# A two-layer model on one core: `weigh` of the second chunk moved behind its scan, and the first step's weight pieces and engine orders changed

## What is computed

```python
zxbcdt = hidden @ W_in                       # 2 x 1024 tokens, 512 -> gate 1024, x 1024, B 16, C 16, dt 16 heads
xBC = silu(conv4(xBC) + conv_b)              # causal, four taps
dt = softplus(dt + dt_bias)
dA = exp(dt * -exp(A_log))
for t: h = h * dA[t] + (dt[t] * x[t]) B[t];  y[t] = h C[t]      # per head, 64 x 16 state
y = (y + D_skip * x) * silu(gate)
y = y * rsqrt(mean(y * y) + 1e-5) * norm_w
out = y @ W_out;  x = layernorm(x + out)
```

## Time and profile before

| | |
|---|---|
| time, median of 3 runs | 1096.6 us (1095.79 to 1098.11) |
| the profiled execution's own time | 1097.13 us |
| its span, first to last instruction | 1095.4 us |
| TensorE busy | 1040.9 us (95%) |
| VectorE busy | 710.6 us (65%) |
| ScalarE busy | 576.1 us (53%) |
| the first layer | the first 400 us: a first step of 61 us, then steps of 48.1 us |
| mean granted clock of TensorE | 0.99 |

### The profile page before, as it was taken

One profiled execution on the slowest core, in us unless ns is written; L12 is line 12 of the kernel. 1 busy time (PEld: TensorE's weight loads), 2 busy tenths in 40 slices (PEclk: granted clock), 3 DMA queues, 4 the chain that ended last, 5 costly groups with the idle time before them and its releaser, 6 DMA issues.

```text
span 1095.4 us, 17774 instructions
## 1 busy us (share of the span) xinstructions
PE 1040.9 (95%) x6784; PEld 911.9 (83%) x6784; DVE 710.6 (65%) x1217; ACT 576.1 (53%) x1189; POOL 343.6 (31%) x465
## 2 busy tenths in 40 slices
PE   5799999999999977999999999899999999999997
PEld 5688889898988966899999999788888888888886
DVE  5999989999998988676677678854341142233123
ACT  7968686776868664566556655663203312321320
POOL 1014324241432415343534353323313312321331
PEclk9999999999999998999999999999999999999999
DMA  7421221404132452401100110435012012001001
GB/s 269 142 91 51 104 98 55 141 11 150 44 110 77 151 166 76 183 1 39 39 25 16 39 39 24 128 110 212 1 48 68 1 39 77 1 13 65 1 1 58
DMA packets 41332, 81.18 MB, mean 74 GB/s; under 512 B 7200, under 2 KB 13216, under 8 KB 39200
## 3 DMA queue, kind: packets, MB, share of 16 engines
q1 hardware_dynamic: 41248, 80.05, 21.6%
HBM read 67.18 MB, written 12.85 MB: 73 GB/s over the span
## 4 chain that ended last, share of the span: by engine, by line
PE 65%; DVE 18%; ACT 7%; issue 4%; POOL 3%; DMA 2%; SPq 0%; DVEq 0%; POOLq 0%; ACTq 0%
PE banks L1859 21%; PE banks L810 17%; PE banks L1872 11%; PE banks L1507 7%; DVE a_L L674 4%; PE banks L1475 4%; DVE c_gx L1366 1%; PE banks L926 1%; DVE c_cv L1342 1%; DVE a_xs L705 1%; DMA c_xb<-tokens 1%; PE banks L874 1%; DVE c_xb L1321 1%; ACT c_a L1241 1%; DVE a_ex L660 1%
## 5 line engine op out<-in xcount | busy, mean ns | idle before, releaser
L1759 ACT ACTIVATE d_sg<-banks,d_gs 128x512 f32<-128x512 f32 x64 | 44.0, 688 | 224.9 <-PE banks L1859 224.9
L1802 DVE SCALAR_TENSOR_TENSOR d_h<-banks,d_us,d_sg 128x512 f32<-128x512 f32 x64 | 48.0, 750 | 163.7 <-PE banks L1859 151.4
L1733 POOL TENSOR_TENSOR d_hl<-d_h,d_hh 128x512 fp32r<-128x512 f32 x64 | 83.4, 1303 | 158.1 <-ACT d_hh L1763 158.1
L1872 PE MATMUL banks<-d_wd,d_hh 128*128 128x512 f32 x256 | 101.1, 395 | 0.0
L1872 PE MATMUL banks<-d_wd,d_hl 128*128 128x512 f32 x256 | 100.9, 394 | 0.0
L649 DVE SCALAR_TENSOR_TENSOR a_xs<-a_xpre,a_cvec,a_xs 128x256 f32<-128x256 f32 x192 | 91.7, 543 | 1.0 <-ACT a_xs L454 1.0
L810 PE MATMUL banks<-a_xth,a_wxh 128*128 128x256 f32 x256 | 74.8, 292 | 2.7 <-DVE a_wxl L585 2.7
L674 DVE TENSOR_TENSOR_SCAN a_L<-a_L,a_ident 128x512 f32<-128x512 f32 x64 | 74.7, 1210 | 0.5
L810 PE MATMUL banks<-a_xth,a_wgh 128*128 128x256 f32 x256 | 74.6, 291 | 0.0
L341 POOL TENSOR_TENSOR a_sg<-a_sg 128x512 f32<-128x512 f32 x16 | 20.6, 1290 | 169.4 <-ACT a_sg L446 169.4
L810 PE MATMUL banks<-a_xtl,a_wxh 128*128 128x256 f32 x256 | 72.6, 284 | 0.0
(11 more groups left out here) (273 smaller groups left out, 3106.6 us busy)
## 6 DMA issues: line engine op xcount, KB each, us to landing
a_L<-decays SPq DMA_DIRECT2D x16, 1024.0 KB, 4.7
a_xf<-in_x_turned SPq DMA_DIRECT2D x16, 256.0 KB, 4.0
a_xr<-in_x SPq DMA_DIRECT2D x16, 256.0 KB, 2.8
tokens<-a_xr SPq DMA_DIRECT2D x16, 256.0 KB, 2.1
c_xb<-tokens SPq DMA_DIRECT2D x16, 256.0 KB, 3.1
d_xin<-tokens SPq DMA_DIRECT2D x16, 256.0 KB, 4.9
d_r<-tokens SPq DMA_DIRECT2D x16, 256.0 KB, 2.6
d_wd_codes<-in_down_w SPq DMA_DIRECT2D x4, 1024.0 KB, 9.4
```

Of the source, the lines that this page charges most:

```text
L1733: pool.tensor_tensor(hl[:, m, :], h32[:, m % 2, :], hh[:, m, :].bitcast(F32), ALU.subtract).then_inc(s_hl, 1)
L1759: act.activation(sg[:, m % 2, :], ps_g[:, m % 2, :], ACT.Silu, scale=gs[:, m:m + 1]).then_inc(s_sg, 1)
L1802: dve.scalar_tensor_tensor(out=h32[:, m % 2, :], in0=ps_u[:, m % 2, :], scalar=us[:, m:m + 1], in1=sg[:, m % 2, :], op0=ALU.mult, op1=ALU. ...
L1872: ins = pe.matmul(ps_o[:, c % 2, :], h[:, m, cols(c)], wd[:, m, :], start=(m == 0 and h is hh), stop=(m == M - 1 and h is hl))
```

## The change

In all steps, `weigh` of the second chunk stands directly behind its scan on VectorE, ahead of `update`, `output` and `conv_bc`. All else is in the first step:

- The pieces of w_x and of the gate's weights are column blocks: piece 1 + p holds the 256 columns that `x_proj(0, p)` needs, with all 512 input rows, in runs of 1 KB. `x_proj(0, p)` and `gate(0, p)` wait for their own piece.
- ScalarE and VectorE split two x pieces, then do `nega`'s exponential and clamp and ScalarE's `bc(0)`, then the other two; the first eviction stands ahead of softplus and decay.
- TensorE turns the steps' dt behind `x_proj(0, 3)`, does `gate(0, 0)` ahead of the first `x_turn`, and `gram(0)` behind it; VectorE takes the turned dt (`steps_in`) behind its third convolution pair.
- The four w_out pieces are split at the end of step 0's order: on ScalarE ahead of `high_y(0)`, on VectorE ahead of `low(0)`.

```diff
--- before.py
+++ after.py
@@ -201,19 +201,18 @@
 
     pieces = [(w_bc.rearrange("(k p) n -> p k n", p=P), wb[0], wb[1], KD, None)]
     for w_dram, w in ((w_x, wx), (w_gate, wg)):
-        for k in range(KD):
-            pieces.append((w_dram[k * P:(k + 1) * P, :], w[0][:, k, :], w[1][:, k, :], 1, None))
+        for p in range(4):
+            own = slice(2 * p * P, (2 * p + 2) * P)
+            pieces.append((w_dram.rearrange("(k p) n -> p k n", p=P)[:, :, own], w[0][:, :, own], w[1][:, :, own], KD, None))
     for m in range(0, M, 2):
         pieces.append((w_out[m * P:(m + 2) * P, :].rearrange("(a p) n -> p a n", p=P), wo[0][:, m:m + 2, :], wo[1][:, m:m + 2, :], 2, m))
-    NX, NG, NW = 1 + KD, 1 + 2 * KD, len(pieces)
+    NX, NG, NW = 5, 9, len(pieces)
     for raw, src, hi, lo in following:
         pieces.append((src, hi, lo, None, None))
     def staged(i):
         w, n = pieces[i][1], pieces[i][3]
         if n is None:
             return following[i - NW][0]
-        if n == 1:
-            return stage[i % 4]
         return stage[i % 4][:, 0:n * w.shape[2]].rearrange("p (a n) -> p a n", a=n)
 
     def chunk(dram, s, j):
@@ -497,17 +496,19 @@
 
         high_piece(0)
         turn(0)
-        for i in range(1, NX):
-            high_piece(i)
+        high_piece(1)
+        high_piece(2)
+        act.wait_ge(s_prep, 1)
+        act.activation(nega, nega, ACT.Exp).then_inc(s_prep, 1)
         act.wait_ge(s_small, 64)
         bc(0)
+        high_piece(3)
+        high_piece(4)
+        act.wait_ge(s_const, 15 + HQ)
+        evict(0, 0)
         softplus(0)
-        act.wait_ge(s_prep, 1)
-        act.activation(nega, nega, ACT.Exp).then_inc(s_prep, 1)
         act.wait_ge(s_prep, 3)
         decay(0)
-        act.wait_ge(s_const, 15 + HQ)
-        evict(0, 0)
         high_piece(NX)
         high_piece(NX + 1)
         evict(0, 1)
@@ -541,9 +542,6 @@
             else:
                 following_stage["turn_in"](0)
                 high_piece(NW)
-            if s == 0:
-                for i in range(NG, NW):
-                    high_piece(i)
             own_heads(C * s)
             if s:
                 normalize(C * s - 2)
@@ -560,6 +558,9 @@
                 evict(s + 1, 1)
             else:
                 following_stage["square"](0)
+            if s == 0:
+                for i in range(NG, NW):
+                    high_piece(i)
             high_y(C * s)
         square(C * NS - 2)
         following_stage["softplus"](0)
@@ -719,14 +720,15 @@
 
         low_piece(0)
         turn(0)
-        for i in range(1, NX):
-            low_piece(i)
+        low_piece(1)
         dve.wait_ge(s_small, 64)
         dve.tensor_scalar(nega, nega, LIMIT, None, ALU.min).then_inc(s_prep, 1)
+        low_piece(2)
         dve.wait_ge(s_prep, 2)
         dve.tensor_scalar(nega, nega, -1.0, None, ALU.mult).then_inc(s_prep, 1)
+        low_piece(3)
+        low_piece(4)
         conv_bc(0)
-        steps_in(0)
         dve.wait_ge(s_const, 15 + HQ)
         for s in range(NS):
             conv_pair(s, 0)
@@ -742,7 +744,9 @@
             else:
                 mean_sq(C * s - 2)
             conv_pair(s, 2)
-            if s:
+            if s == 0:
+                steps_in(0)
+            else:
                 residual(C * s - 2)
             conv_pair(s, 3)
             scan(C * s, 0)
@@ -761,16 +765,13 @@
             else:
                 following_stage["turn_in"](0)
                 low_piece(NW)
-            if s == 0:
-                for i in range(NG, NW):
-                    low_piece(i)
             scan(C * s + 1, 1)
+            weigh(C * s + 1)
             update(C * s)
             output(C * s, 0)
             output(C * s, 1)
             if s + 1 < NS:
                 conv_bc(s + 1)
-            weigh(C * s + 1)
             mix(C * s + 1, 0)
             mix(C * s + 1, 1)
             if s + 1 == NS:
@@ -779,6 +780,9 @@
             update(C * s + 1)
             output(C * s + 1, 0)
             output(C * s + 1, 1)
+            if s == 0:
+                for i in range(NG, NW):
+                    low_piece(i)
             low(C * s)
             if s + 1 < NS:
                 steps_in(s + 1)
@@ -855,8 +859,8 @@
             pe.matmul(ps_q[:, j:j + 1], sg[:, 0, cols(j)], ones, start=True, stop=True).then_inc(s_sp, 1)
 
         def x_proj(s, p):
-            if s == 0 and p == 0:
-                pe.wait_ge(s_wlo, NX)
+            if s == 0:
+                pe.wait_ge(s_wlo, 2 + p)
             if p < 2:
                 wait(pe, s_sg, 4 * (s - 1) + p + 3)
             else:
@@ -875,8 +879,8 @@
             last.then_inc(s_xtr, 1)
 
         def gate(s, p):
-            if s == 0 and p == 0:
-                pe.wait_ge(s_wlo, NG)
+            if s == 0:
+                pe.wait_ge(s_wlo, NX + 1 + p)
             if p < 2:
                 pe.wait_ge(s_acc, M * s + 2 * p + 6)
             else:
@@ -931,7 +935,6 @@
         pe.wait_ge(s_wlo, 1)
         bc(0)
         x_proj(0, 0)
-        turn_steps(0)
         x_proj(0, 1)
         for s in range(NS):
             x_proj(s, 2)
@@ -940,16 +943,20 @@
                 out_proj(C * s - 2, 1)
                 sum_sq(C * s - 2)
             x_proj(s, 3)
-            gram(s)
             if s:
+                gram(s)
                 out_proj(C * s - 1, 0)
-            x_turn(s, 0)
-            if s:
+                x_turn(s, 0)
                 out_proj(C * s - 1, 1)
-            x_turn(s, 1)
-            gate(s, 0)
-            if s:
+                x_turn(s, 1)
+                gate(s, 0)
                 sum_sq(C * s - 1)
+            else:
+                turn_steps(0)
+                gate(0, 0)
+                x_turn(0, 0)
+                gram(0)
+                x_turn(0, 1)
             x_turn(s, 2)
             gate(s, 1)
             x_turn(s, 3)
```

## The result

13 executions of each: before 1098.11 us median (1095.79 to 1100.08), after 1094.38 us (1092.06 to 1096.08). The ratio is 0.9970, 95% interval 0.9962 to 0.9978: 3.3 us faster, between 2.4 and 4.2. The forecast was a change of 5.2 us. Its absolute figure, 1091.9, counted from an execution of 1097.1; here the kernel before has a median of 1098.1, so I judge the change and not the level.

The account below looks back on a forecast made before the run. TensorE was taken to bound the steady steps, with one hole at L903's wait for `a_bw`, but not the first step. Steps -6.0 plus first step +0.8 gave -5.2 us, from 1097.13 to 1091.9 us; range 1087.8 to 1095.0.

Parts of the forecast that it names:

- Part 1, the steps: Steps 1 to 6: `weigh` moved ahead starts L903 1.0 us earlier per step, 6.0 us won; bounds 3.0 and 5.6.
- rival B: Steady steps: another wait takes over and half the gain is lost; -2.2 us, 1094.4 us; chance 0.12.
- Part 2, to the second eviction: First step's start: first eviction at 15.0 instead of 19.34, second ending 23.5 against 24.27; with late loads, nothing won.
- rival C: The start is late through slow 1 KB runs and a first projection wholly at 1.2 GHz; 1093.9 us; chance 0.10.
- The term for the loads: Start: small loads behind the pieces in 1 KB runs land up to 1.4 us late; 0.7 taken.
- The extra table load of part 2: ScalarE's start: `nega`'s Exp ahead of Softplus makes Exp's table load twice, 1.28 us a load.
- Part 3, to the gates: End of the first step's gates: turn of the next x comes 1.0 us earlier; bounds 0 and 1.9.
- Part 4, the late split: First step, w_out split later: L903 6.9 us earlier, first output matmul 0.9 earlier; with 1.7 for the clock, 0.8 worse.
- the step "0.9 won" at the first output matmul: First step: first output matmul starts at 70.6 against 71.61, 0.9 us won, between 0 and 2.8.
- The clock term: Behind TensorE's 6 us stand ahead of the first output matmul: half speed for 3.4 us, costing 1.7 us.
- Rival D: First step: the late w_out split costs more than it frees; +1.7 us, 1098.3 us with no head start; chance 0.04.
- The table load: ScalarE: the skill page adds 1.38 us drain per table switch, making the sum 1.4 worse; the trace showed no drain.

Follow-up runs that it names:

- experiment 2: The changed kernel with `weigh` put back behind `conv_bc`, so the changed start alone; ratio 1.0004 against the kernel before.
- 1: The kernel before with only `weigh` of the second chunk moved directly behind its scan; ratio 0.9948 against the kernel before, 5.7 us faster.
- 11: The kernel before with `weigh` moved and 30 overwritten matmuls in the 3.72 us stand ahead of `bc` of step 1; ratio 0.9933 against the kernel before.
- A: The kernel with the whole change; median 1094.38 us, ratio 0.9970 against the kernel before.
- 10: The kernel before with `weigh` moved and all four w_out pieces split late, nothing else; ratio 0.9968 against the kernel before.
- 5: The changed kernel with two of the four w_out pieces split earlier, behind `own_heads` (ScalarE) and `weigh` (VectorE); ratio 0.9944 against the kernel before.
- 6: The changed kernel with step 1's fourth x projection ahead of the first output product; ratio 0.9953 against the kernel before.
- experiment 3: The changed kernel with the four w_out pieces split in their old place; ratio 0.9948 against the kernel before.
- 4: The changed kernel plus 44 overwritten matmuls in the stand ahead of the first output matmul; ratio 0.9945 against the kernel before.
- 7: The changed kernel with two w_out pieces split earlier and step 1's fourth x projection ahead of the first output product; ratio 0.9923 against the kernel before.
- 12: As 7, with `gram(0)` again ahead of the first `x_turn` and `steps_in(0)` ahead of the third convolution pair; ratio 0.9926 against the kernel before.

## Why the prediction was right or wrong

**Part 1, the steps: right.** Forecast 6 x 1.0, measured 5.45, 0.91 each; the lower bound from the modelled ends (0.93) was nearer. The wait is gone in every step, with no other in its place (rival B is out), and step 0 shows none either. VectorE's wait for TensorE, 1.94 us in the earlier trace rows, sums to 7.5 us in seven steps where it was 13.5: 0.86 less in each, so VectorE did follow.

**Part 2, to the second eviction: an early term was wrong.** I had the first projection end by 14.5 "at the fast clock". It ran straight behind `bc` with matmuls 0.21 us apart until 15.2, and the eviction waited until 16.58, not 15.0. The second one ended at 25.31, against 24.27 and the forecast's 24.2: rival C's mechanism at 1.1 us. The loads were as late as I took them: the last small one landed at 12.2 (6.67 and 5.5) against 11.5, 0.7, though TensorE's first matmul was itself 0.25 later. But they set nothing: ScalarE was through with its copies by 15.46 and then stood 1.12 us for the projection. The term for the loads had no part in the time. The runs of 1 KB themselves were dearer, between the forecast's two bounds: from 5 to 12 us the DMA moved 302 GB/s at a share of 1.00, and 304 at 0.90 before, which is 302 and 338 at full share.

The extra table load of part 2 never came. ScalarE has six loads in the first 62 us of either trace; `nega`'s exponential ran at 12.38 with none between the load at 0.80 and softplus's at 18.11. That cost the forecast nothing, since the exponential waited for the small load in any case.

**Part 3, to the gates: wrong in sign.** Forecast 1.0 earlier; the turn of the next x began at 48.55 against 47.64, 0.9 later. The fourth eviction was 1.0 late from part 2, and ScalarE then stood 1.72 for `gram` (1.3 foreseen). The gate block done ahead gave ScalarE's later waits back, 1.2 and 0.9 down to 0.3, and that covered only `gram`. On VectorE the first scan began at 34.78, not at 33.5, for the same 1.0 of the fourth eviction. The term also left out a new stand: TensorE's fourth projection waited 3.29 us for the second eviction (row of 25.45), and the clock was at half behind it (granted 0.51 from 25.5 to 29.0).

**Part 4, the late split: the mechanism was foreseen, the step "0.9 won" at the first output matmul failed.** L903 came at 56.43, not at 54.5: 5.0 won instead of 6.9, all of it the 1.9 that parts 2 and 3 missed. From there the sum held: the lows took 5.38, `high_y` began at 69.79, and with `low` at 1.23 the output matmul began 15.7 us behind L903, 16.1 forecast. So it was 0.55 late instead of 0.9 early. The stand was 5.40, 6 forecast. The clock term, 1.7, measured 2.1 to 2.2. Together the first step gave +2.7 in the traces, against +0.8. And not all of the 5.0 is the late split's: 2.17 of it was L903's wait for `a_bw`, which moving `weigh` removes by itself (experiment 2).

Against medians the whole lost 1.9 of the 5.2, not the 2.5 that the traces' terms would make (0.55 from the steps, 1.9 from the first step). The stand of 3.72 us can account for such a difference (experiments 1 and 11): behind it the clock falls in most traces, and in the one that I read it did not. That it does account for it was not measured.

**Rival D** had the right place and asked the wrong question: the late split did outweigh the freed wait, by 2.2 us, though L903 came 5.0 earlier. I weighed it against the six steps, where it could not win, and not against `weigh` alone. The forecast treated parts 1 and 4 as one sum; the better question was what part 4 is worth beside part 1. By the forecast's own terms the answer was there: the old place cost a 3.72 us stand, the new one a stand of 6 and the clock.

**The table load.** The load for softplus, at 18.11 to 19.39, is followed by its activation at 19.41: no drain of 1.38 us, as the earlier trace rows had it and against the Trainium skill ("ScalarE: Activation LUTs", What ACT_TABLE_LOAD costs).

## What to carry to other kernels

An operation that only the next engine's product needs belongs right behind its inputs, ahead of what merely could run; find it by the wait that recurs once a step, and test it alone. Work taken out of one engine's stand must go where no one waits: four pieces at one place cost 2.2 us, two and two with a projection between left a stand of 0.15 us. And price a stand of TensorE by its length and by the clock behind it; where it can't be avoided, fill it with TensorE's own later work, or even with matmuls for nothing.

## What the runs showed of the hardware

Behind a stand the clock falls in one execution and not in another. After 5.40 us it fell in all three traces that have such a stand (A, 2, 10), after 3.72 us in three of four, after 2.99 and 2.64 us (5, 6) in the one trace of each. TensorE then worked at 1.2 GHz for 3 to 6 us, after the same 5.40 us for 3.2 (2), 4.4 (A) and 5.9 (10).

The first 45 us differ as much. Around A's stands of 1.08 and 1.50 us at 35 to 38 us the clock held, as in experiment 3; in experiments 2, 4 to 7 and 12, which have them too (12 only the second), it fell. Experiments 4 and 6 run A's program up to L907. From the first matmul to it are 47.13 us in A (mean granted clock 0.96), 49.47 and 49.60 in them (0.86 both). So A's trace had a good first step, and the 5.0 us that L907 won in it may be more than an average execution shows. Over A's 13 executions the mean granted clock goes from 0.980 to 0.989. The highest is that of the fastest (1092.06 us), but the two of 0.980 took 1094.1 and 1094.2: the mean does not order the rest.

The granted clock reads 1.00 in the first microseconds even where the matmuls run at half speed. A's window of 9 to 15 us:

```profile
9.00:15.00 6.00, 5.70 (x27) 5.73 (x28) 3.35 (x6) 3.84 (x7) 0.00 (x0) 1.00 0.78 233
```

27 matmuls of 256 columns start in 5.7 us, 0.21 apart; from 15.4 on they start 0.12 apart. Early in a trace the spacing tells the speed and the column does not.
